# Writing out the first step of a state-space mixer kernel: no work on step -1, weights and x split between projections

## The reference

```
proj = x @ W_in.T ; val, gate, Bp, Cp, dt = split(proj)
val  = silu(causal_conv4(val) + conv_b)
ld   = softplus(dt + dt_bias) * -exp(A_log)
cum  = cumsum(ld over the tokens of a sequence)
Y    = ((C B^T) * exp(cum_l - cum_m), causal) @ val + D * val     # 32 heads of width 16, state 128
out  = (Y * silu(gate)) @ W_out.T                                  # added to x
```

## Time and profile before

| | us |
|---|---|
| median of 3 runs (lowest, highest) | 863.64 (862.07, 865.16) |
| the profiled execution, its own time | 863.73 |
| the span in its trace | 861.9 |
| PE busy | 758.5 (88%) |
| VectorE busy | 636.6 (74%) |
| ScalarE busy | 437.3 (51%) |
| GpSimd busy | 345.8 (40%) |

### The profile page before, as it was taken

How to read it: one execution, slowest core, us unless ns; L and a number is a source line. 1 busy time by engine, 2 the same in 40 slices (tenths; PEclk the granted TensorE clock), 3 DMA queues, 4 the chain that set the end, 5 groups by cost and what they waited for, 6 DMA issues and landing times. The chain is left out here.

```text
span 861.9 us, 18011 instructions
## 1 busy us (share of the span) xinstructions
PE 758.5 (88%) x5790; PEld 403.6 (47%) x5795; DVE 636.6 (74%) x1094; ACT 437.3 (51%) x790; POOL 345.8 (40%) x349
## 2 busy tenths in 40 slices
PE   4699999999999999999999999954689999695773
PEld 1355555555555555555555555533233333243342
DVE  5578677678686687686686887867777778648995
ACT  6444445744455744444754444424367777542333
POOL 5573443754243835333753543316020000105572
PEclk8799999999999999999999999975799999998997
DMA  6721111331211151111112112011140000014411
GB/s 212 309 83 70 76 49 49 113 143 49 96 50 49 50 205 49 49 73 73 49 49 97 49 49 94 4 25 33 24 179 19 19 13 20 6 52 163 179 49 49
DMA packets 23332, 66.13 MB, mean 77 GB/s; under 512 B 7024, under 2 KB 11632, under 8 KB 17648
## 3 DMA queue, kind: packets, MB, share of 16 engines
q1 hardware_dynamic: 23312, 65.90, 20.9%
HBM read 62.55 MB, written 2.42 MB: 75 GB/s over the span
## 5 line engine op out<-in xcount | busy, mean ns | idle before, releaser
L241 POOL TENSOR_TENSOR cum_rows<-cum_rows,cum_t 128x512 f32<-128x512 f32 x128 | 135.8, 1071 | 203.8 <-DMA cum_rows<-cum_scratch 203.8
L560 PE MATMUL pring<-xt_hi,w_hi 128*128 x576 | 172.9, 382 | 6.1 <-DVE gate L485 4.5
L560 PE MATMUL pring<-xt_lo,w_hi 128*128 x576 | 172.3, 381 | 0.0
L560 PE MATMUL pring<-xt_hi,w_lo 128*128 x576 | 171.9, 380 | 0.0
L461 DVE TENSOR_TENSOR bt<-pring,bt 128x512 f16<-128x512 f32 x128 | 88.0, 687 | 73.6 <-ACT bt L333 73.5
L333 ACT CAST bt<-pring 128x512 f16<-128x512 f32 x128 | 74.5, 582 | 129.1 <-PE pring L560 128.9
L465 DVE TENSOR_TENSOR ct<-pring,ct 128x512 f16<-128x512 f32 x128 | 87.9, 687 | 52.9 <-ACT ct L337 52.6
L572 PEld LDWEIGHTS pscore<-ct,bt 128*128 128x128 f16 x1548 | 96.1, 98 | 34.9 <-issue 8.9
L572 PE MATMUL pscore<-ct,bt 128*128 128x128 f16 x1548 | 107.6, 219 | 1.7 <-issue 0.8
L813 DVE TENSOR_REDUCE mx<-bank_at 128x4 f32<-128x512 f32 x128 | 83.1, 677 | 28.3 <-PE bank_at L904 28.0
L337 ACT CAST ct<-pring 128x512 f16<-128x512 f32 x128 | 74.7, 583 | 54.4 <-PE pring L560 54.4
(11 more groups left out here) (153 smaller groups left out, 945.9 us busy)
## 6 DMA issues: line engine op xcount, KB each, us to landing
cum_rows<-cum_scratch SPq DMA_DIRECT2D x32, 1024.0 KB, 4.6
w_raw<-in_w_in SPq DMA_DIRECT2D x36, 256.0 KB, 5.4
weight_b<-weight_scratch SPq DMA_DIRECT2D x8, 1024.0 KB, 6.7
mt<-in_xt SPq DMA_DIRECT2D x4, 512.0 KB, 6.8
acc<-in_x SPq DMA_DIRECT2D x1, 2048.0 KB, 12.0
vals<-in_vals SPq DMA_DIRECT2D x16, 128.0 KB, 2.0
out<-acc SPq DMA_DIRECT2D x4, 512.0 KB, 2.9
w_raw_e<-in_w_up SPq DMA_DIRECT2D x1, 1024.0 KB, 5.0
```

The source lines that it names most:

```text
L241: nc.gpsimd.tensor_tensor(rows[:, par, q], rows[:, par, q], own, ALU.subtract).then_inc(sem("since"), 1)
L560: mm = nc.tensor.matmul(bank[name][:], w[:, c, k, cols], x[:, k, bass.ds(n % TB, 1), :].rearrange("p o n -> p (o n)"), start=(i == 0), sto ...
```

## The change

- **First step.** Each of PE, VectorE, ScalarE gets a `first_step` of its own; the loops start at n = 1. What belongs to step -1 is gone from it: scores, weighing and `outputs` of slot -1, `add_skip`, `gate_y`, `high_y`, `low_y`, `out_project`, `add_out`. The zero fills go, except for `val_pad`; semaphores are primed by `sem_inc`.
- **Splits.** ScalarE splits chunks 0 and 1 ahead of the step, chunk 2 after the softplus and each further one between evacuations. GpSimd splits token blocks 2 and 3 of x (high and low), and its low parts of the weights are put between its exponents. PE waits for block 0 of x alone before it starts.
- **Softplus.** |dt + bias| moves to ScalarE (Abs with bias, out of PSUM), the rate is folded into two VectorE operations, four instructions in all on VectorE as before but in another order.
- **Sums.** They go by token block: the dt matmuls write `pscore` with sequences on the partitions' quarters and token blocks along the columns, so that one running sum of 128 columns gives block 0, and three more follow within step 0. The turn and the copy are split in the same way, and the store to DRAM is 4 + 4 DMAs where it was one.
- **W_out** has a buffer of its own and is loaded with the weights. `x` and `expo` are loaded behind the rows of step 0.
- **Queues.** `wdt`, `dtb`, chunks 0 and 1, `cw`, `ident` and `dskip` are issued by ScalarE. On SP the rows of step 1 are issued ahead of the next group's weights.

More of the change, by code:

```diff
@@ L410, in _, with sums @@
[L410 to L415, removed]
+            def sums(t):
+                s = slice(t * L, t * L + L)
+                nc.vector.tensor_tensor_scan(dz[:, 0, s], ones[:, s], dz[:, 3, s], 0.0, ALU.mult, ALU.add).then_inc(sem("dt_cum"), 1)
@@ L486, in step, with val_silu, pad_values, first_step @@
                                                op0=ALU.add, op1=ALU.mult).then_inc(sem("gate_silu"), 1)
+            def val_silu(n):
+                dve.wait_ge(sem("val_tanh"), n + 1)
+                nc.vector.scalar_tensor_tensor(out=val_t[:], in0=th_val[:], scalar=1.0, in1=conv_h[:].rearrange("p b n -> p (b n)"),
+                                               op0=ALU.add, op1=ALU.mult).then_inc(sem("val_silu"), 1)
+            def pad_values(n):
+                dve.wait_ge(sem("val_turned"), n + 1)
+                t = bank["T"][:].rearrange("p (b q r d) -> p b q r d", b=NB, q=4, r=2)
+                for par in range(2):
+                    c = nc.vector.tensor_copy(val_pad[:, par, :, :, par * HD:par * HD + HD], t[:, :, :, par, :])
+                c.then_inc(sem("val_pad"), 1)
+            def first_step():
+                convolve(0, 0)
+                convolve(0, 1)
+                dve.wait_ge(sem("dt_log"), 3)
+                dve.wait_ge(sem("dt_z"), 2)
+                nc.vector.scalar_tensor_tensor(out=dz[:, 3, :], in0=dz[:, 3, :], scalar=rate[:, 1:2], in1=dz[:, 0, :],
+                                               op0=ALU.mult, op1=ALU.add).then_inc(sem("dt_rate"), 1)
+                dve.wait_ge(sem("dt_rate"), 2)
+                sums(0)
+                convolve(0, 2)
+                convolve(0, 3)
+                gate_silu(0)
+                low_b(0, 0)
+                low_c(0, 0)
+                sums_turned(0, 1)
+                low_b(0, 1)
+                val_silu(0)
+                low_c(0, 1)
+                sums(1)
+                low_b(0, 2)
+                sums(2)
+                low_c(0, 2)
+                sums(3)
+                low_b(0, 3)
+                low_c(0, 3)
+                sums_turned(1, TB)
+                weigh(0, 0)
+                weigh(0, 1)
+                weigh(0, 2)
+                pad_values(0)
+                for s in range(4, SLOTS):
+                    low_b(0, s)
+                    low_c(0, s)
+                    weigh(0, s - 1)
+            def step(n, norm=False):
+                convolve(n, 0)
+                weigh(n, -1)
+                for k in range(1, 4):
+                    convolve(n, k)
+                gate_silu(n)
                 low_b(n, 0)
@@ L491, in step @@
                 low_b(n, 1)
-                dve.wait_ge(sem("val_tanh"), n + 1)
-                nc.vector.scalar_tensor_tensor(out=val_t[:], in0=th_val[:], scalar=1.0, in1=conv_h[:].rearrange("p b n -> p (b n)"),
-                                               op0=ALU.add, op1=ALU.mult).then_inc(sem("val_silu"), 1)
+                val_silu(n)
                 low_c(n, 1)
@@ L505, in step @@
                 weigh(n, 2)
[L506 to L510 removed]
+                pad_values(n)
                 for s in range(4, SLOTS):
@@ L607, in turn_values, with pair, first_step, step @@
                 mm.then_inc(sem("val_turned"), 1)
-            with pe.Fori(0, STEPS) as n:
+            def pair(n, s):
+                project(n, f"B{s}", s + 1, 0, "b_proj")
+                project(n, f"C{s}", s + 1, 1, "c_proj")
+            def first_step():
+                project(0, "val", 0, 0, "val_proj", "xt_lo", 1)
+                project(0, "gate", 0, 1, "gate_proj")
+                pair(0, 0)
+                pair(0, 1)
+                turn_sums(0, 1)
+                scores(0, 0)
+                pair(0, 2)
+                scores(0, 1)
+                pair(0, 3)
+                turn_sums(1, TB)
+                scores(0, 2)
+                turn_values(0)
+                for s in range(4, SLOTS):
+                    pair(0, s)
+                    scores(0, s - 1)
+                    if s == 5:
+                        outputs(0, 0)
+                pe.wait_ge(sem("xt_lo"), 2)
+                pe.wait_ge(sem("xt_late"), 4)
+            def step(n):
                 project(n, "val", 0, 0, "val_proj")
@@ L625, in _ @@
                         outputs(n, 0)
+            first_step()
+            with pe.Fori(1, STEPS) as n:
+                step(n)
             scores(STEPS, -1)
```

239 lines of the change are left out of this document (146 added, 93 removed).

## The result

The changed kernel takes 850.46 us (median of 4 runs, 849.75 to 855.4), the kernel before 863.05 in the runs beside it. The ratio is 0.9863, 95% interval 0.9821 to 0.9906: 1.4% faster, where 853.8 was forecast. A repeat on another occasion gave 851.32 against 864.09, ratio 0.9860 (0.9811 to 0.9908).

A forecast was written before the change was run, and what follows sets the result against it. PE bounds the mixer from step 1 on, so the gain is step 1's earlier start: head 13.2 less 3.3 taken back in step 0, 9.95 off 863.73, giving 853.8. Own range 850 to 858, overall 848.5 to 859.5.

The forecast's parts named there:

- Head, -13.2: Time ahead of step 0: `val` would start at 11.9 where it was 25.1.
- The last block of x lands at 11.3: Load of x in the head: last block lands at 11.3 as before, give or take 0.7, with about the same bytes ahead.
- 0.5 us after the last block: dt matmuls in the head: packed on four quarters, done 0.5 us after x's last block, at worst 1.7.
- VectorE's low x at 11.6: VectorE's low part of x in the head: done at 11.6, so not holding back `val` at 11.9.
- the walk: Engine-by-engine timeline of step 0: PE stands 4.6 ahead of C0, 2.9 ahead of B3, 2.8 ahead of scores 2.
- Step 0, 44.2: Length of step 0: 44.2 us where it was 40.95, taking back 3.3 of the head's gain.
- The half clock: PE's clock in step 0: half speed after the 4.6 us wait; 0.5 added for the two later gaps.
- Removed work: PE's work in step 0: 3.1 us dropped and 0.4 added, 32.69 becoming 30.0 us.
- W_out: Old step 0: PE's 4.5 us wait for `gate_silu` was ScalarE's list held up by W_out's load ahead of `th_gate`.
- GpSimd's costs: GpSimd in step 0: copy of 1024 with cast taken as 1.85, between 0.955 and 2.13; contention with VectorE no more than occasional.
- The contention rival: GpSimd's chain in step 0 at its longest values, +6.5, step 1's first exponent late: 858 to 861.5; chance 0.14.
- After step 0, nothing: Steps after step 0, attention and experts: no change; slack of 1.3 us before step 1's first exponent is asked for.

The follow-up runs named there:

- x_vec: The changed kernel with ScalarE and VectorE splitting all four blocks of x ahead of step 0, GpSimd none; 851.18 us, ratio 0.9846 to the kernel before.
- small_first: The changed kernel with ScalarE issuing the loads of cw, ident and dskip ahead of chunks 0 and 1; 855.0 us, ratio 0.9887 to the kernel before.
- sp_queue: The changed kernel with every load issued by SP in the order of the kernel before; 855.67 us, ratio 0.9890 to the kernel before.
- less_gpsimd: The changed kernel with block 3 of x off GpSimd, high parts of chunks 6 to 8, first decay and weighing earlier, low chunk 5 later; 844.29 us, ratio 0.9771.
- sums_whole: The changed kernel with all four running sums in one row ahead of the second conv step, turned and copied at once; 850.61 us, ratio 0.9839.
- head_weights: The changed kernel with ScalarE splitting chunks 2 to 8 ahead of step 0, as before; 851.6 us, ratio 0.9851 to the kernel before.

## Why the prediction was right

The time, 850.46, is inside both ranges, though near the low end of the narrower one (850 to 858). The frame of the sum, the one number "where does step 1 start", held: 56.1 forecast, 55.80 and 55.12 measured. Inside it two terms were off by about 3 us each, against each other, so that it came out this close is partly luck.

- **Head, -13.2: mis-sized, -10.6 measured.** The 2.6 us are three terms. "The last block of x lands at 11.3" failed: its matmuls start at 12.71 (1.4 late). The step put the bytes as equal; with every load on SP they start at 11.47, so chunks 0 and 1 beside x cost 0.6 to 1.2 us. "0.5 us after the last block" failed: the 16 dt matmuls take 1.08 (0.6 more), as long as 32 of 128 columns take in `outputs` at 47.22, so they ran at half the pace that the step took from `outputs`. "VectorE's low x at 11.6" failed too: it stood behind a wait for `dskip`, which ended at 12.73, and PE waited 0.7 more for it. This is a wait that the walk had not priced.

```profile
47.22 1.08 PE L697 MATMUL py<-mt,val_pad 128*32 128x128 f32 x32
```

```profile
12.73 0.36 DVE L471 TENSOR_SCALAR cw<-cw 128x16 f32<-128x16 f32 x1 [4.99 <-DMA dskip<-in_dskip]
...
13.14 1.21 DVE L455 TENSOR_TENSOR xt_lo<-mt,xt_hi 128x1024 f16<-128x1024 f32 x1
...
15.37 1.26 DVE L479 TENSOR_SCALAR dz<-dz,rate 128x512 f32<-128x512 f32 x1
...
20.00 0.42 DVE L460 TENSOR_TENSOR_SCAN dz<-ones,dz 128x128 f32<-128x128 f32 x1
...
28.32 1.74 DVE L460 TENSOR_TENSOR_SCAN dz<-ones,dz 128x128 f32<-128x128 f32 x1
```

- **Step 0, 44.2: 41.3 and 40.5 measured.** Four waits are there in their places; their sizes: ahead of C0 0.4 to 0.6 in place of 4.6; for C2's bank 1.9 (2.9); ahead of scores 2 3.1 (2.8); B7's for a low part 0.6 (B7 at 52.3 forecast, 52.55 measured). The first shrank because `val` started late and at half clock, while the convolution chain hangs on dt: C0 was forecast at 20.4 and came at 21.89. So 2.6 us of late head became 1.5 at C0, and B3 came at 31.93, 1.0 earlier than forecast: there VectorE's list, from the copy of the turned sums to low C2, took 5.8 us where the walk had 6.5. `x_vec` shows the other side: with the chain 1.5 us longer, C0 waits 3.7.
- **The half clock** cost 2.9 us at the start (three projections from 14.50 to 21.3, where the walk had 3.9 us at full clock and gave no reason for it), and nothing at C0, for which the walk had 2.55 us in place of 1.3; behind scores 2 it came, at 1.3 where the walk had 0.5.
- **Removed work** of 3.1 us: the walk left it out without a price of its own. Put back it cost 1.2 to 2.0.
- **W_out**: the prediction named the wait of 4.5 us and its cause, without a term of its own; alone it is worth 5.6 to 5.8, the wait plus the clock. Cause right.
- **GpSimd's costs**: the copy took 1.04, near the lower end (1.85 taken); the contention of the Trainium skill's rule (GPSIMD Engine Reference, 1. Specifications), which I left as "occasional", is regular, but VectorE pays it too. GpSimd's subtraction of 1024 took 3.20 and 2.45 on x where it takes 2.13 on W_out. The contention rival did not come: on the chain of step 0 a low part took 1.15 to 1.27, a subtraction 1.04 to 1.17 and a cut about 0.63, none near the longest values that its 6.5 us were made of.
- **After step 0, nothing**: the slack was there, but the later steps came out 1.3 us shorter on average, a gain that the prediction did not have. With it the gain that the traces place is 12.0; between the medians it is 12.6 to 12.8, 2.6 to 2.8 above the forecast.

## What to carry to other kernels

Find the first point from which the bound engine runs without a wait, and price each edit ahead of it by what it moves that point; then read that point from the trace, where it varied by 0.7 us between two traces of the changed kernel, and not from the times alone, which in the same kernel went from 847.6 to 856.3. Walk each engine's list in its written order: `small_first` and `sp_queue` lost 3.3 to 5.0 us to a load of 1 KB or a chunk that an engine's list waited for ahead of something else. Look for what the orders of the engines still hold back: `less_gpsimd`, with one block of x off GpSimd, block 0 of x, the high parts, the first decay and weighing forward, gained 3.7 to 4.3 us more, where x's split, the weights and the sums by block are worth 0.4 to 3.0 each.

## What the runs showed of the hardware

- **An operation of VectorE that starts beside one of GpSimd can be held until that one ends.** A sum of 128 columns took 0.42 us with GpSimd idle (at 20.00 above), 1.74 from 28.32 to 30.06, beside this subtraction, which ends at 29.78:

```profile
27.33 2.45 POOL L229 TENSOR_TENSOR xt_lo<-mt,xt_hi 128x1024 f16<-128x1024 f32 x1
```

  In the kernel before, four sums took 1.24 each, beside low parts of the weights at 1.19 each (seven in 8.35 us). It hits a one-input operation too: `dz * rate` takes 0.49 alone, 1.26 at 15.37 above, and 2.36 from 17.04 to 19.40 in `small_first`, with a subtraction of GpSimd from 17.00 to 19.13. In these cases (1.74, 1.26 and 2.36) the operation ends 0.3 us behind GpSimd's. GpSimd can be the one that pays: at 13.14 both began a subtraction of x, VectorE's took 1.21, as with GpSimd idle at 16.55, and GpSimd's 3.20. Operations of VectorE that read PSUM kept their length beside GpSimd (low B2 and low C2 0.66 each, at 29.98 and 31.21).
- **The length of the half clock at the start varies.** At the same place, behind the same matmuls, it lasted from 2.4 us (`less_gpsimd`) over 2.9 (`x_vec`) and 4.3 (`sums_whole`) to 6 (`head_weights` and the changed kernel). What sets it no run here tells.
- **Packing paid.** With the four sequences on four quarters of the columns, the dt matmuls of a block of x took 1.08 us where they took 7.07 for four blocks before, 1.77 each. In the kernel before, they filled PE from 6.2 to 13.3, and PE started each block as it landed; now PE is busy for 4.3 of the 7.5 us from 6.33 to 13.8. The first projections come at 1.2 GHz in both kernels: before, behind waits of 4.2 and 4.8 us, now behind such thin work and a wait of 0.7; whether more of it would have raised the clock was not tried.
